# A small language-model layer on one core: where the gathers of the first chunk are issued, and where they land

## What is computed

```
h = w0[ids] @ w1                       # gather of rows of 512, product to 256
h = h * (ids != 0) * 256 ** 0.5
h = h + attn(layernorm(h))             # two layer norms, token shift and mix, k/v/r products,
                                       # WKV recurrence, channel mix (256 -> 1024 -> 256)
h = h + ffn(layernorm(h))              # fp4 quantise; gate and up 256 -> 704, down 704 -> 256
```

## Time and profile before

| | us |
|---|---|
| median of three runs | 747.94 (747.89 to 749.3) |
| the profiled execution | 747.51 |
| its span, first to last instruction | 745.7 |
| TensorE busy | 716.9 (96%) |
| VectorE busy | 589.2 (79%) |
| ScalarE busy | 510.0 (68%) |
| GpSimd busy | 154.9 (21%) |

### The profile page before, as it was taken

One profiled execution on the slowest core, in us unless ns is written; L12 is line 12 of the kernel. 1 busy time (PEld: TensorE's weight loads), 2 busy tenths in 40 slices (PEclk: granted clock), 3 DMA queues, 4 the chain that ended last, 5 costly groups with the idle time before them and its releaser, 6 DMA issues.

```text
span 745.7 us, 10723 instructions
## 1 busy us (share of the span) xinstructions
PE 716.9 (96%) x3702; PEld 602.9 (81%) x3702; DVE 589.2 (79%) x1031; ACT 510.0 (68%) x893; POOL 154.9 (21%) x220
## 2 busy tenths in 40 slices
PE   6998899899999999999999999999999999899987
PEld 5858767797789968897789868896889878898876
DVE  0687969786988789787998799787998698883685
ACT  2674997488858896589757995689748885663231
POOL 2304401430034201530043201620052002200200
PEclk9999999999999999999999999999999999999999
DMA  4801100100002000100011000100010000000000
GB/s 128 286 2 29 29 0 2 28 30 1 15 9 63 1 1 15 43 29 1 15 41 31 1 1 15 56 16 1 14 43 1 1 14 1 15 1 15 15 1 29
DMA packets 13377, 19.39 MB, mean 26 GB/s; under 512 B 982, under 2 KB 10764, under 8 KB 13324
## 3 DMA queue, kind: packets, MB, share of 16 engines
q1 hardware_dynamic: 10720, 10.31, 4.3%
q0 software_dynamic: 2560, 8.39, 3.8%
q10 hardware_dynamic: 44, 0.01, 0.0%
HBM read 14.51 MB, written 4.19 MB: 25 GB/s over the span
## 4 chain that ended last, share of the span: by engine, by line
PE 78%; DVE 11%; ACT 5%; issue 3%; DMA 1%; POOL 1%; DVEq 0%; ACTq 0%; POOLq 0%
PE psB L570 20%; PE psC L645 15%; PE psB L600 11%; PE psC L672 10%; PE psA L561 9%; PE psA L531 6%; PE psC L660 2%; PE psA L519 1%; PE psC L504 1%; DMA rows<-L_tok_w,ids_now 1%; DVE mix L1000 1%; PE psB L541 1%; DVE mix L1025 1%; PE psC L629 1%; DVE scales L1180 1%
## 5 line engine op out<-in xcount | busy, mean ns | idle before, releaser
L570 PE MATMUL psB<-cwv_s,kkT 128*128 128x256 f32 x512 | 113.2, 379 | 0.7 <-ACT kkT L858 0.7
L570 PEld LDWEIGHTS psB<-cwv_s,kkT 128*128 128x128 f32 x512 | 96.6, 190 | 16.8 <-issue 2.9
L561 PE MATMUL psA<-mix,kvr_s 128*128 128x512 f32 x192 | 86.4, 593 | 3.0 <-DVE mix L1000 1.8
L645 PE MATMUL psC<-up_hi,xq_hi 128*128 128x352 f32 x256 | 85.9, 335 | 2.1 <-DVE xq_lo L1273 1.5
L452 POOL TENSOR_SCALAR sc_c<-mv_c 128x2 f32<-128x2 f32 x16 | 7.6, 474 | 384.7 <-DVE mv_c L1163 384.7
L672 PE MATMUL psC<-downT,hqT 128*128 128x256 f32 x384 | 85.9, 380 | 0.1
L645 PE MATMUL psC<-up_hi,xq_lo 128*128 128x352 f32 x256 | 82.6, 323 | 0.0
L645 PE MATMUL psC<-up_lo,xq_hi 128*128 128x352 f32 x256 | 82.5, 322 | 0.0
L672 PEld LDWEIGHTS psC<-downT,hqT 128*128 128x128 f32 x384 | 72.2, 190 | 10.3 <-ACT hqT L923 0.5
L561 PEld LDWEIGHTS psA<-mix,kvr_s 128*128 128x128 f32 x192 | 36.1, 190 | 40.3 <-issue 36.3
L1000 DVE SCALAR_TENSOR_TENSOR mix<-hT,rest,mix 128x512 f32<-128x512 f32 x80 | 54.5, 748 | 16.3 <-ACT mix L774 16.3
(11 more groups left out here) (170 smaller groups left out, 1561.6 us busy)
## 6 DMA issues: line engine op xcount, KB each, us to landing
out<-h SPq DMA_DIRECT2D x16, 256.0 KB, 2.1
mix<-L_attn_cwk SPq DMA_DIRECT2D x1, 1024.0 KB, 10.4
cwv_s<-L_attn_cwv SPq DMA_DIRECT2D x1, 1024.0 KB, 13.2
hq<-L_ffn_w_gate SPq DMA_DIRECT2D x1, 704.0 KB
hq<-L_ffn_w_up SPq DMA_DIRECT2D x1, 704.0 KB, 6.7
hqT<-L_ffn_w_down SPq DMA_DIRECT2D x1, 704.0 KB, 10.2
w_s<-L_tok_w SPq DMA_DIRECT2D x1, 512.0 KB, 3.6
rows<-L_tok_w,ids_now POOLq DMA_INDIRECT x32, 4.0
```

The lines of the kernel that those rows point to most:

```text
L561: mm = nc.tensor.matmul(psA[:, A.slot(f"{name}{d}")], kvr_s[:, w, k, d * P:(d + 1) * P], mix[:, w, k].rearrange("p c t -> p (c t)"), start ...
L570: mm = nc.tensor.matmul(psB[:, B.slot(name), q * D:(q + 1) * D], lhsT[:, k, (2 * j + q) * P:(2 * j + q + 1) * P], weight[:, k, :], start=( ...
L645: mm = nc.tensor.matmul(psC[:, C.slot(name), f, 0:INTER // 2], a[:, k, t * P:(t + 1) * P], b[:, w, k, f * (INTER // 2):(f + 1) * (INTER // ...
```

## The change

For chunk 0 alone, all four gathers are issued in `gather(0)`, one after the other. Those of tiles 2 and 3 go into the first part of `mix` (seen as two tiles of 128 x 512, called `first`) and count on two semaphores of their own (`first_in`). `gather(1)` returns at once for chunk 0. TensorE's `turn_a(1)` of chunk 0 reads `first` and waits for `first_in`. All later waits for `rows_in` are lower by one gather. SyncE's second wait, ahead of the large weights, is for `first_in`. Later chunks are gathered as before.

```diff
--- before.py
+++ after.py
@@ -251,6 +251,7 @@
         takev = sb("takev", [P, H, CS, ROW])
         y = takev[:].rearrange("p h c r -> p (h c r)")[:, 0:TILES * D].rearrange("p (t d) -> p t d", d=D)
         e_new, numer = mix[:, 0], mix[:, 1]
+        first = mix[:, 0].rearrange("p h c t -> p (h c t)").rearrange("p (q e) -> p q e", e=E)
         attT = rT
 
 
@@ -318,6 +319,7 @@
 
         ids_cut = signal("ids_cut", 2)
         rows_in = [sem(f"rows_in{q}") for q in range(2)]
+        first_in = [sem(f"first_in{q}") for q in range(2)]
         a_full, a_act = signal("a_full", len(A_JOBS)), signal("a_act", len(A_JOBS))
         A = Jobs(A_JOBS, a_full, {"act": a_act})
         b_full, b_act, b_dve = signal("b_full", 16), signal("b_act", 12), signal("b_dve", 4)
@@ -395,7 +397,7 @@
             for k, w in enumerate((wk, wv, wr)):
                 sp.dma_start(kvr_s[:, k], w.rearrange("(k p) d -> p k d", p=P)).then_inc(s_kvr, 16)
             for q in range(2):
-                sp.wait_ge(rows_in[q], 32)
+                sp.wait_ge(first_in[q], 16)
             for k, w in enumerate((w_gate, w_up)):
                 sp.dma_start(raw_up[:, k * GJ:(k + 1) * GJ, :], w.rearrange("n (h d) -> (n h) d", h=H).rearrange("(j p) d -> p j d", p=P)).then_inc(s_raw[k], 16)
             sp.dma_start(raw_down, w_down.rearrange("(h p) n -> p h n", p=P)).then_inc(s_raw[2], 16)
@@ -437,6 +439,8 @@
                         nc.gpsimd.tensor_copy(ids_now[:, s, :], ids_col[:, 0, here]).then_inc(ids_cut.sem, 1)
                         nc.gpsimd.tensor_copy(mask_now[:, s, :], ids_col[:, 1, here]).then_inc(ids_cut.sem, 1)
                         hold(pool, ids_cut, ch, 2)
+                    elif ch.base == 0:
+                        return
                     else:
                         hold(pool, a_full, ch, A.names.index("xt1") + 1)
                     for q in range(2):
@@ -444,6 +448,11 @@
                         pool.indirect_dma_start(rows[:, q, :], None, tok_w0,
                                                 bass.IndirectOffsetOnAxis(ap=ids_now[:, s, t:t + 1], axis=0)
                                                 ).then_inc(rows_in[q], 16)
+                    if ch.base == 0:
+                        for q in range(2):
+                            pool.indirect_dma_start(first[:, q, :], None, tok_w0,
+                                                    bass.IndirectOffsetOnAxis(ap=ids_now[:, s, 2 + q:3 + q], axis=0)
+                                                    ).then_inc(first_in[q], 16)
                 return step
 
             def coefficients(ch, sc, mv, coef, done=0):
@@ -513,11 +522,15 @@
                 def step(ch):
                     warm(f"a_turn{j}", ch, psB[:, 1])
                     for t in (2 * j, 2 * j + 1):
-                        pe.wait_ge(rows_in[t % 2], ch.times(32, 16 * (j + 1)))
+                        if ch.base == 0 and j:
+                            pe.wait_ge(first_in[t % 2], 16)
+                        else:
+                            pe.wait_ge(rows_in[t % 2], 16 if ch.base == 0 else ch.times(32, 16 * j))
                         A.wait_free(pe, ch, f"xt{t}")
                         for k in range(KE):
                             mm = nc.tensor.transpose(psA[:, A.slot(f"xt{t}"), k * P:(k + 1) * P],
-                                                     rows[:, t % 2, k * P:(k + 1) * P], ident[:])
+                                                     (first if ch.base == 0 and j else rows)[:, t % 2, k * P:(k + 1) * P],
+                                                     ident[:])
                         mm.then_inc(a_full.sem, 1)
                 return step
 
```

## The result

Seven runs of the changed kernel beside seven of the one before: median 745.11 us (744.25 to 746.32) against 749.3 us (747.76 to 749.45). The ratio is 0.9957 with a 95% interval of 0.9945 to 0.9969: the change makes the kernel 3.2 us faster (2.3 to 4.1). The medians themselves lie 4.2 us apart, because the runs of each kernel fall into two groups (before: three from 747.76 to 747.94, four from 749.3 to 749.45; after: four from 744.25 to 745.11, three from 745.64 to 746.32) and a median takes the larger one; what follows goes by the ratio. Forecast were 1.92 us and 746.0 us. The profiled execution took 744.41 us, its span 742.6 against 745.7.

The account below looks back on a forecast made before the run. It took TensorE, busy 96% of a 745.7 us span, to bound the run, with chunk 0's set-up a relay. The 747.94 us median less 1.92 us gave 746.0 us, other terms costing nothing; range 745.2 to 747.9.

Parts of the forecast that it names:

- 1.92 us: Chunk 0's relay: product 1 starts at 16.76 instead of 18.68, and the whole run ends that much earlier.
- The wait for the bank of product 0: Tile 3's transposes wait for ScalarE to empty product 0's PSUM bank at 16.12, so start at 16.17, not 18.19.
- The last step: Before product 1: ScalarE's copy of tile 2 ends at 16.71, later than tile 3's bound of 16.66; start 16.76.
- rival A: Four gathers in flight crowd each other; a full collision starts product 0 2.50 us later, giving 748.5 us; chance 0.06.
- The cover of 2.0 us: Gather 4 lands at 14.15 against its need at 16.17 for tile 3's transposes.
- Cwk's request: SyncE's wait ahead of the large weights ends near 14.2 instead of 18.2, so their requests move about 4 us earlier.
- cost nothing: At ScalarE's cast: cwk lands at 28.8, or 30.0 at the slower rate, before its need at 30.06.
- rival B: Cwk lands after 30.06 and holds ScalarE's cast, cutting the gain to as little as 0.2 us, 747.7 us; chance 0.12.
- No cost, no gain: TensorE's granted clock is 1.00 in each stretch read, so the clock term was taken as nothing.
- D: A later stage gives back part of the first chunk's gain; between 746.7 and 748.0 us; chance 0.08.
- the row at 54.60: One chunk 1 gather took GpSimd 3.64 us to issue while VectorE was busy; the others took 0.95.
- rival C: GpSimd issues the gathers slowly, so gather 4 lands at 18.91, 0.77 us later than before, 748.7 us; chance 0.02.

Follow-up runs that it names:

- the clean pair: The kernel before with both TensorE gaps filled, 746.23 us, and the changed kernel with its late gap filled, 744.21 us, on one chip.
- late_weights: The changed kernel, but SyncE requests the large weights only when tile 3 is transposed; 747.51 us, ratio 0.9991.
- after_g1: The changed kernel, but gathers 3 and 4 wait until gather 1 has landed; 746.83 us, ratio 0.9973.
- after_shift: The changed kernel, all some 1.3 us later (two memsets ahead of the first gather, 14 more warming transposes); 747.57 us, ratio 0.9986.
- base_again: The kernel before, unedited, run once more; 747.77 us, ratio 0.9999.
- late_issue: The changed kernel with its buffer and semaphores, but gathers 3 and 4 wait again until tile 1 is transposed; 748.92 us, ratio 1.0005.
- start_before: The kernel before with only its start gap on TensorE (15.2 to 17.1 us) filled by 16 warming transposes; 748.15 us, ratio 0.9998.
- gap_after: The changed kernel with 24 identity transposes filling TensorE's late gap; 744.14 us, ratio 0.9943.
- gap_after_2: The changed kernel with TensorE's late gap filled, run again on another occasion; 744.21 us.
- gap_late_weights: The changed kernel with the late gap filled and the large weights requested only when tile 3 is transposed; 744.8 us, ratio 0.9953.
- gap_before: The kernel before with 24 identity transposes in TensorE's late 3.29 us gap; 746.1 us, ratio 0.9975.

## Why the prediction was right, and where not

**The relay.** From the start of product 0 to that of product 1 I worked out 5.19 us (11.57 to 16.76); it is 5.17 (11.89 to 17.06), and 5.16 or 5.17 in five further traces of the changed order. The wait for the bank of product 0 sets it, as forecast: ScalarE had emptied it 4.55 us after product 0's start, to the hundredth. The last step was another than mine, and here two errors cancel. I had tile 3 begin 0.05 us behind ScalarE and the copy of tile 2 come last; in the trace tile 3 began 0.14 us behind it, and product 1 0.48 us behind that (17.06), while the copy was done at 16.92. On the other side the late order took 7.11 us in the trace that I had, and 6.95 to 7.31 in five others whose clock was full there, 7.18 in the mean of the six. So the gain of 1.92 us was right in mechanism and size: 2.0 by the mean, 2.1 in the clean pair.

**Gather 2.** Forecast: tile 1 at 11.08 as before. It came at 11.40, which is why the first pair of traces shows only 1.55 us of relay. This isn't rival A. With two gathers in flight the seven traces have tile 1 between 11.08 and 11.44 (mean 11.25), with four in flight the five unshifted ones between 11.17 and 11.58 (mean 11.38). The difference of the means is 0.1 us, in a scatter of 0.4, so a delay by the company isn't shown beyond that; the trace of before was the quickest of its kind.

**Gather 4 and the weights.** It landed at about 15.0, not by 14.15: I took 4.36 us beside other transfers, it was 5.2 with four gathers and the kvr weights together. The cover of 2.0 us was 1.6, enough. Cwk's request, forecast 4 us earlier, came 2.3 us earlier (19.41 for 21.71), as gather 4 was late and the w_down request took 3.25 us instead of 2.36. It was still in time, so "cost nothing" holds, but by less than I thought; rival B's mechanism is real, and late_weights shows what it costs where it comes (0.6 to 0.9 us).

**The step that failed: the clock.** "No cost, no gain" rested on stretches up to 40 us, where the granted clock was 1.00. But the page's mean was 0.998, and 0.002 of 745 us at half speed is one stretch of some 3 us somewhere else. A look at the stretches up to 150 us would have found it behind the longest gap after the opening wait, at 136, and a question for the change. It is the missing term of the sum, 1.1 us: 3.2 measured less 2.1 of relay, and 0.2 to 2.0 by the interval of the ratio. Counted by runs it would be about 1.6, from 1.46 steps of the mean clock (one in each run of the kernel before, a second in 46%) to 0.43 (three runs of seven), at 1.5 us each. How large it is in the long run isn't settled: late_weights, after_g1 and after_shift, which have the early issue too, had 1.000 in only five of 33 runs. It also made my range too narrow below: the median of 745.11 lies 0.1 us under its end. The two groups of runs, 747.9 and 749.3 to 749.4, stood in the times too: I took 749.3 for scatter. That 746.0 still came within 0.9 us of the measured median is in part luck. It started from 747.94, while the median of seven runs before was 749.3, and the size of the gain was missed by 1.3 us.

**Rivals C and D** didn't come: each of the four issues took 0.94 to 1.23 us, and what the relay gives stays to the end. On the row at 54.60 that rival C leans on: what VectorE ran beside that issue were two-input TENSOR_TENSORs, the last of them until 57.24, and the issue ended at 58.24, 1.00 us later, about the length of one undisturbed issue (0.95 us). That looks like a hold-up until their end, but no run here tests it.

**What stays open.** Why the late stretch of half clock goes in some runs, though its gap of 3.29 us is the same. Shown is that it does: of the kernel before, base_again and late_issue none of 93 runs had 1.000, of the changed kernel four of seven. Early issue isn't needed for it, as start_before had one such run in 12. What the kernels with such runs share is that TensorE sits idle for less between product 0 and product 1: 0.6 to 1.3 us in the traces of start_before, after_g1, late_weights, after_shift and the changed kernel (ten of 52 runs at 1.000, with the late gap open), 2.1 to 2.5 us in those of the other three. That is a count, not a cause; no experiment takes it apart. The Trainium skill ("TensorE: Matmul & The Clock Gate", section "Part 1: The HAM clock gate") says that the window in which the chip judges TensorE's activity runs freely and isn't reset at a kernel's start. That the same kernel falls in some runs and not in others agrees with it; that it comes in each of 93 runs of three nearly equal kernels doesn't follow from it, and no run here explains it. Nor is shown what the runs at 0.995 of start_before lost, or where the stretch lies in the three of 17 runs of gap_after, gap_after_2 and gap_late_weights that had 0.998.

## What to carry to other kernels

Follow a chain of waits to the wait that is late next, and sum up from there: issuing the transfers 4 us earlier gave 2.1 us, because the emptying of a PSUM bank came next, and it kept them only because the weights behind moved along (0.6 to 0.9 us otherwise). Read the granted clock over the whole span before forecasting a small gain: a mean of 0.998 was a stretch at half clock that cost 1.5 us here, nearly as much as the relay gave. Where TensorE waits as long as here (3.29 us) in the middle of a run, try to fill the wait rather than warm up behind it: in the kernel before it gave 1.9 us (ratio 0.9975), and the changed kernel with its gap filled took 744.14 us and 744.21 us, the shortest medians of all versions here. Against the 745.11 us of the changed kernel that is a hint only, as they weren't run beside it and the intervals of their ratios overlap.

## What the runs showed of the hardware

In six traces a gap of 3.29 us on TensorE was followed by a granted clock of 0.50 for some 3 us of unbroken work, although 34 warming transposes stood directly behind it; in the trace of the changed kernel it wasn't. Warming behind such a gap pays at the lower clock (5.56 for 3.90 us); in the gap it cost nothing that the times show. Gaps of 1.91 us (base_again) and 2.04 us (gap_before) were followed by such a stretch too, one of 1.95 us (before) was not. A stretch can have double length: 6.7 us in after_shift. The mean clock of a run tells how long it stood at half clock, and not how many stretches that was; it splits the times of one program into groups 1.5 us apart.
